# Preparation stage of a two-layer network: four places for contexts and heads, another order of the first loads, statistics split around the root

## The reference

```python
x = x + _L0_xattn_ref(_layernorm(x), ctx_512, ...)      # 16 heads
# in _L0_xattn_ref:
q_hk = (hidden_q @ Wq.T).reshape(b, s, H, K)
q_big = einsum('bshk,hkq->bshq', q_hk, w_kc_q)
kv_rope = kv_c * cos[None] + _rotate_half(kv_c) * sin[None]
q_r = einsum('bshq,hqr->bhsr', q_big, W_qr)
k_r = einsum('bld,hdr->bhlr', kv_rope, W_kr)
scores = einsum('bhsr,bhlr->bhsl', q_r, k_r);  attn = softmax(scores)
ctx_c = einsum('bhsl,bld->bhsd', attn, kv_rope)
out = einsum('bhsd,hkd->bshk', ctx_c, w_kc_kv).reshape(b, s, H * K) @ Wo.T
x = x + _L0_ffn_ref(_layernorm(x), ...)                 # ternary weights
x = x + _L1_xattn_ref(_layernorm(x), ctx_512, ...)      # causal attention
x = x + _L1_ffn_ref(_layernorm(x), ...)                 # 8 of 32 experts
```

## Time and profile before

| what | us |
|---|---|
| three runs | 1895.8, 1899.0, 1899.07 (median 1899.0) |
| the profiled execution | 1894.58 |
| its span | 1892.7 |
| `prepare` in it | 0 to 125.6 |
| busy in the span: TensorE, VectorE, ScalarE, GpSimd | 1615.2, 1223.4, 1058.8, 641.3 |

### The profile page before, as it was taken

The page is one execution under the profiler, slowest core; times in us unless marked ns, Lnnn a source line. Parts: engine busy times, 40 slices in busy tenths (PEclk is TensorE's granted clock), DMA queues, the critical chain, the costliest instruction groups (busy, mean ns, idle before and its releaser), DMA issues. The chain is left out here.

```text
span 1892.7 us, 36294 instructions
## 1 busy us (share of the span) xinstructions
PE 1615.2 (85%) x12180; PEld 1033.0 (55%) x12199; DVE 1223.4 (65%) x2744; ACT 1058.8 (56%) x2661; POOL 641.3 (34%) x479
## 2 busy tenths in 40 slices
PE   5588999999999889989998777655489999999993
PEld 4455656656646645545554455443356666666562
DVE  5666796796796787787787767766833333333332
ACT  3347846746746727565675776642645555555452
POOL 4523403403404400000000222211067777777672
PEclk7779999999999999999999998776589999999997
DMA  7730130130120139786677001011446665656536
GB/s 232 264 128 9 35 90 12 35 90 12 34 90 12 38 119 345 243 302 199 222 256 238 28 2 37 27 36 47 118 90 134 146 139 130 156 117 153 129 76 219
DMA packets 143366, 226.62 MB, mean 120 GB/s; under 512 B 37887, under 2 KB 93439, under 8 KB 143062
## 3 DMA queue, kind: packets, MB, share of 16 engines
q1 hardware_dynamic: 107190, 195.90, 32.7%
q0 software_dynamic: 29344, 21.29, 6.9%
q10 hardware_dynamic: 6656, 7.11, 1.1%
HBM read 175.00 MB, written 98.80 MB: 145 GB/s over the span
## 5 line engine op out<-in xcount | busy, mean ns | idle before, releaser
L2741 PE MATMUL g_ps<-ring,xT 128*128 x1572 | 300.7, 327 | 1.0 <-issue 1.0
L1012 POOL TENSOR_TENSOR pr<-pr,sm 100x1444 f32<-100x1444 f32 x64 | 166.2, 2596 | 367.9 <-DVE sm L1044 367.9
L2690 POOL DMA_INDIRECT acc<-rows,slot_sources x131 | 207.8, 1586 | 107.2 <-issue 77.0
L2847 DVE SCALAR_TENSOR_TENSOR hf<-sg,g_ps 128x192 f32<-128x192 f32 x131 | 46.4, 354 | 236.4 <-ACT sg L2796 189.0
L2741 PEld LDWEIGHTS g_ps<-ring,xT 128*128 128x128 f16 x1572 | 142.3, 98 | 72.3 <-issue 6.9
L2680 POOL DMA_INDIRECT xg<-xtab,slot_sources x131 | 138.4, 1056 | 81.8 <-issue 79.9
L1039 DVE TENSOR_REDUCE sm<-s_banks 100x2 f32<-100x722 f32 x128 | 115.8, 905 | 76.0 <-PE s_banks L783 75.5
L2763 PE MATMUL d_ps<-ring,hT 128*128 x655 | 162.8, 379 | 2.0 <-issue 1.3
L936 ACT ACTIVATE pr<-s_banks,sm 100x361 f32<-100x361 f32 x256 | 142.2, 567 | 34.1 <-DVE sm L1039 30.0
L783 PE MATMUL s_banks<-kvp,qp 128*100 128x361 f16 x768 | 138.6, 317 | 9.1 <-ACT pr L936 4.7
L840 PE MATMUL o_bank<-cT,N_hi 128*128 128x400 f16 x512 | 129.4, 335 | 1.9 <-ACT tern_a L615 0.8
(11 more groups left out here) (328 smaller groups left out, 3873.8 us busy)
## 6 DMA issues: line engine op xcount, KB each, us to landing
split_f<-in_gu SPq DMA_DIRECT2D x64, 384.0 KB, 4.5
split_gu<-split_o SPq DMA_DIRECT2D x64, 384.0 KB, 3.1
ring<-split_gu SPq DMA_DIRECT2D x32, 768.0 KB
head<-in_head SPq DMA_DIRECT2D x16, 864.0 KB, 6.4
tern_w<-in_tern SPq DMA_DIRECT2D x48, 256.0 KB, 3.2
split_f<-in_down SPq DMA_DIRECT2D x32, 384.0 KB, 4.2
split_d<-split_o SPq DMA_DIRECT2D x32, 384.0 KB, 3.7
ring<-split_d SPq DMA_DIRECT2D x32, 256.0 KB
```

The source lines that it names most:

```text
L1012: nc.gpsimd.tensor_tensor(pr[:, s % 3], pr[:, s % 3], small[:, s % 3, 2, :].unsqueeze(2).to_broadcast([SEQ, 4, KEYS]), ALU.mult).then_inc( ...
L2690: nc.gpsimd.indirect_dma_start(out=core.acc[i % NACC][:, :], out_offset=bass.IndirectOffsetOnAxis(ap=core.sources[:, i:i + 1], axis=0), in ...
L2741: last = nc.tensor.matmul(g_ps[i % 2][:, 0:2 * INTER], xT[:, i % 2, a * KT + k, :], ring(i, (2 * k + w) * 2 * INTER, 2 * INTER), start=((k ...
```

## The change

Contexts and heads get four places each (2 and 3 before). SP asks for rows of chunk 0 ahead of head 0, for those of chunk 1 behind context 2, and for those of chunk c+2 at b = 4c+1. A chunk's next statistics are split: `before_root` runs behind the moments in pass 2 of the chunk, the root stands ahead of `ln.high` on ScalarE in pass 3, and `after_root` is where the whole was. The moments stay.

```diff
--- before.py
+++ after.py
@@ -293,14 +293,14 @@
     core.gate = (w["gateT"], w["alpha"])
     assert BATCH == HEADS
     DQT = DCQ // P
-    NH = 3
+    NH, NK = 4, 4
     core.first_stage()
     x_even, x_odd, tab_in, kr_in = (core.sem(n) for n in ("x_even_in", "x_odd_in", "rope_tables_in", "kr_in"))
     kr_hi = core.sem("kr_hi_done")
 
-    kv_in = Slots(core, "kv_in", 2, per=16)
-    prod, roped = Steps(core, "rope_products", per=3, depth=2), Steps(core, "kv_roped")
-    lat_turned, turned = Steps(core, "latent_turned", depth=2), Steps(core, "kv_turned", depth=2)
+    kv_in = Slots(core, "kv_in", NK, per=16)
+    prod, roped = Steps(core, "rope_products", per=3, depth=NK), Steps(core, "kv_roped")
+    lat_turned, turned = Steps(core, "latent_turned", depth=NK), Steps(core, "kv_turned", depth=2)
     hi, lo = Steps(core, "kv_hi", per=3), Steps(core, "kv_lo", per=3, depth=2)
     saved = Slots(core, "kv_saved", 2, per=32, depth=1)
 
@@ -311,7 +311,7 @@
     with ExitStack() as ctx:
         cos = core.sb(ctx, "rope_cos", [P, 3, DC], F32)
         sin = core.sb(ctx, "rope_sin", [P, 3, DC], F32)
-        kv = core.sb(ctx, "kv_stage", [P, 2, 3, DC], F32)
+        kv = core.sb(ctx, "kv_stage", [P, NK, 3, DC], F32)
         a = core.sb(ctx, "rope_a", [P, 2, 3, DC], F32)
         s = core.sb(ctx, "rope_s", [P, 2, 3, DC], F32)
         r = core.sb(ctx, "kv_rope", [P, 2, 3, DC], F32)
@@ -345,10 +345,10 @@
 
             @block.sync
             def _(sp):
-                def load_context(b, p):
+                def load_context(b):
                     sp.wait_ge(lat_turned.sem, lat_turned.room(b))
                     sp.wait_ge(prod.sem, prod.room(b))
-                    sp.dma_start(kv[:, p], w["ctx"][b]).then_inc(kv_in[p].sem, 16)
+                    sp.dma_start(kv[:, b % NK], w["ctx"][b]).then_inc(kv_in[b % NK].sem, 16)
 
                 def load_head(h):
                     if h >= NH:
@@ -363,21 +363,26 @@
                     sp.dma_start(core.x_rows[:, c * CB:(c + 1) * CB, :],
                                  w["x"][c * CB:(c + 1) * CB].rearrange("b s d -> s b d")).then_inc(arrived, 16)
 
-                load_context(0, 0)
+                load_context(0)
                 sp.dma_start(cos[:, :, :], w["cos"]).then_inc(tab_in, 16)
                 sp.dma_start(sin[:, :, :], w["sin"]).then_inc(tab_in, 16)
+                load_rows(0)
                 load_head(0)
-                load_rows(0)
-                load_context(1, 1)
+                load_context(1)
                 load_head(1)
+                load_context(2)
+                load_rows(1)
                 load_head(2)
+                for h in range(3, NH):
+                    load_head(h)
+                load_context(3)
                 for b in range(BATCH):
-                    if b + 2 < BATCH:
-                        load_context(b + 2, b % 2)
+                    if b + NK < BATCH:
+                        load_context(b + NK)
+                    if b % CB == 1 and b // CB + 2 < NCH:
+                        load_rows(b // CB + 2)
                     if b + NH < BATCH:
                         load_head(b + NH)
-                    if b % CB == 0 and b // CB + 1 < NCH:
-                        load_rows(b // CB + 1)
                     if b == BATCH // 2:
                         sp.dma_start(kr[:, :, :], w["krT"]).then_inc(kr_in, 16)
                 for p in range(2):
@@ -393,12 +398,13 @@
                 for i in range(BATCH // 2):
                     for p in range(2):
                         b = i * 2 + p
-                        pool.wait_ge(kv_in[p].sem, kv_in[p].after(i))
-                        nc.gpsimd.tensor_tensor(a[:, p], kv[:, p], cos[:, :, :], ALU.mult).then_inc(prod.sem, 1)
-
-                        nc.gpsimd.tensor_tensor(s[:, p, :, 0:half], kv[:, p, :, half:DC], sin[:, :, 0:half],
+                        k = b % NK
+                        pool.wait_ge(kv_in[k].sem, kv_in[k].after(b // NK))
+                        nc.gpsimd.tensor_tensor(a[:, p], kv[:, k], cos[:, :, :], ALU.mult).then_inc(prod.sem, 1)
+
+                        nc.gpsimd.tensor_tensor(s[:, p, :, 0:half], kv[:, k, :, half:DC], sin[:, :, 0:half],
                                                 ALU.mult).then_inc(prod.sem, 1)
-                        nc.gpsimd.tensor_tensor(s[:, p, :, half:DC], kv[:, p, :, 0:half], sin[:, :, half:DC],
+                        nc.gpsimd.tensor_tensor(s[:, p, :, half:DC], kv[:, k, :, 0:half], sin[:, :, half:DC],
                                                 ALU.mult).then_inc(prod.sem, 1)
                         pool.wait_ge(prod.sem, prod.after(b))
                         pool.wait_ge(turned.sem, turned.room(b))
@@ -412,10 +418,11 @@
 
             @block.tensor
             def _(pe):
-                def turn_latent(i, b, p):
-                    pe.wait_ge(kv_in[p].sem, kv_in[p].after(i))
+                def turn_latent(b, p):
+                    k = b % NK
+                    pe.wait_ge(kv_in[k].sem, kv_in[k].after(b // NK))
                     pe.wait_ge(lo.sem, lo.room(b))
-                    nc.tensor.transpose(lat_cols(p), kv[0:SEQ, p, 0, :], core.ident[0:SEQ, 0:SEQ]
+                    nc.tensor.transpose(lat_cols(p), kv[0:SEQ, k, 0, :], core.ident[0:SEQ, 0:SEQ]
                                         ).then_inc(lat_turned.sem, 1)
 
                 def turn_keys(b, p):
@@ -448,7 +455,7 @@
                 pe.wait_ge(core.made, IDENT_MADE)
                 for n in range(BATCH):
                     p = n % 2
-                    turn_latent(n // 2, n, p)
+                    turn_latent(n, p)
                     turn_keys(n, p)
                     if n:
                         ln.turn(pe, n, p)
@@ -491,10 +498,10 @@
                 for n in range(BATCH):
                     p = n % 2
                     context_hi(n // 2, n, p)
+                    if n % CB == CB - 1 and n + 1 < BATCH:
+                        ln.root(act, n // CB + 1)
                     if n:
                         ln.high(act, n, p)
-                    if n % CB == CB - 1 and n + 1 < BATCH:
-                        ln.root(act, n // CB + 1)
                     inner_hi(n, p)
                     save_context(n, p)
                     outer_hi(n, p)
@@ -537,7 +544,7 @@
                     if bi < CB - 1:
                         ln.norm(dve, n + 1, 1 - p, bi + 1)
                     elif n + 1 < BATCH:
-                        ln.statistics(dve, c + 1, taken=True)
+                        ln.after_root(dve, c + 1)
                         ln.norm(dve, n + 1, 1 - p, 0)
 
                 for n in range(BATCH):
@@ -556,6 +563,8 @@
                         dve.wait_ge((x_odd, x_even)[c % 2], 16 * ((c + 1) // 2 + 1))
                         for j in (2 * bi - 2, 2 * bi - 1):
                             ln.moments(dve, (c + 1) * CB + j, j)
+                        if bi == 2:
+                            ln.before_root(dve, c + 1)
                     if n == BATCH - CB - 1:
                         dve.wait_ge(kr_hi, 1)
                         nc.vector.scalar_tensor_tensor(core.kr_lo[:, :, :], kr[:, :, :], KR_SCALE,
```

## The result

Before: median 1898.45 us (1895.8 to 1899.07). Changed: median 1883.51 us (1880.32 to 1886.34). The ratio is 0.9918 with a 95% interval of 0.9900 to 0.9936, that is 12 to 19 us faster. The forecast was 1880 us, with a range of 1869 to 1892.

A forecast was written before the change was run, and what follows sets the result against it. Late loads in bursts were taken to hold up the first stage. -21.1 + 4.9 - 3.2, with 2 us given back, made -17.4: 1894.6 to 1877.2, plus 2.8 for the median, 1880 us; eight in ten from 1869 to 1892.

The forecast's parts named there:

- Part 1: First stage: four context places and earlier rows of x remove TensorE's context waits and both holes; 21.1 us gained.
- the lower bound of 10.5: First stage, earlier loads: the bursts only move and half the waits stay; 10.5 us gained.
- the sentence on what hides the loads: First stage: the rest of it hides the loads, DMA share 82% against 0.87 where TensorE is not held up.
- Part 2: First pass: head 0 waits behind rows of chunk 0, so the pass starts 4.9 us later.
- The landing at 7.8: Start of stage, before the change: head 0, issued at 3.0, lands 4.8 us later, at 7.8.
- the rows' 2.9 us at 279 GB/s: First pass, low bound: rows ahead of head 0 take 2.9 us; it lands at 10.7, 0.8 us lost.
- Part 3: Chunk ends: split statistics let ScalarE's root run sooner, 1.06 us gained three times, 3.2 us.
- The 8.4 us at the upper end of its range: Chunk ends: upper end for the split statistics; TensorE waits 8.4 us at three places for ScalarE's g.
- The 2 us given back: First stage: 2 us off the gain, for dense loads and VectorE work about as long as a fast pass.
- Rival 1: First stage: loads are the bound, holes fill with other waits, half of Part 1 and Part 3 remains; 1890 us, 17%.
- Rival 2: First stage: the clock stays up, against granted 0.63 and 0.72 in and after the first hole; 14%.
- Rivals 3 and 4: First pass: head 0 waits, nothing comes back, 1902 us, 5%; or another limit at the same places, 1897 us, 6%.

The follow-up runs named there:

- e2: The changed kernel without the split of the statistics, all small VectorE operations together at the chunk end; 1889.2 us, ratio 0.9954 to the kernel before.
- e11: The kernel before with only rows of x of chunk 0 asked for ahead of head 0; 1897.4 us, ratio 1.0019.
- e12: The changed kernel with four places for saves and without the split of the statistics; 1878.3 us, ratio 0.9914 to the kernel before.
- e1: The changed kernel with head 0 asked for ahead of rows of chunk 0 again; 1880.5 us, ratio 0.9919 to the kernel before.
- e6: The changed kernel with four places instead of two for saved split contexts; 1876.7 us, ratio 0.9894 to the kernel before.
- e10: The changed kernel with head 0 first, four save places, GpSimd held before context 2 until first rows are normalised; 1873.3 us, ratio 0.9907.

## Why the prediction was right, and where its terms were not

**The total.** -17.4 was forecast for the stage; it was -15.0 in the traces and -14.9 in the medians.

**Where it is won.** Right: everything comes from the first stage; no wait for rows and, on TensorE, none for contexts after pass 0; and no hole over 4 us (TensorE's longest wait after 30 us is 3.0). Rest and stage were kept apart correctly: the forecast has no term for the rest, and the 2.9 us seen there lie in a scatter of 11.

**Part 1, "So TensorE's waits for contexts and rotated contexts go, both holes with them": 21.1 us.** The waits went, but not the time. Compare passes of e2 (parts 1 and 2) with e11 (part 2): 101.4 to 91.2, which is 10.2 us, about the lower bound of 10.5. Most of the other half turned into a wait that I never priced, as the 8.4 us show that e12 wins on e2 with more places for saves. ScalarE needs its save buffers back after two passes, and without the holes it comes back for them sooner than a save lands. The save issued at 54.84 lands 10.5 us later, and pass 7 stands:

```profile
54.84 0.54 ACTq L473 DMA_DIRECT2D lat_parts<-lat_parts_sb  x1
...
63.99 0.25 DVE L222 TENSOR_SCALAR ln_t<-ln_t 100x4 f32<-100x4 f32 x1
65.41 0.52 ACT L478 ACTIVATE kv_parts_sb<-kv_rope 128x384 f16<-128x384 f32 x1 [4.88 <-DMA lat_parts<-lat_parts_sb]
...
66.35 0.21 ACT L238 ACTIVATE ln_t<-ln_t 100x4 f32<-100x4 f32 x1
...
66.83 0.23 ACT L487 ACTIVATE g<-gc_ps 128x64 f32<-128x64 f32 x1
```

The small operations were through at 64.24 and the root could have run then; it waited for its turn behind the save until 66.35. With four places for saves (e12 against e11) part 1 is 101.4 to 82.8, 18.6 us: most of the 21.1. The failing step is the sentence on what hides the loads: I compared shares of the DMA engines (0.82 against 0.87) and left out who waits for the transfers in the other direction. A mean share told nothing of this landing: it is 0.78 over the stage, and 1.02 in 55:65, while the save is under way. The landings were hardly shorter before: 10.4 us at the most (in pass 0), and 9.8 and 9.7 in the two holes, where nobody was in a hurry. What holds a landing back for 10 us is not shown; no run here tells an order among the transfers from a plain share of the engines.

**Part 2, 4.9 us.** Mechanism right, size high. Head 0 was used at 14.0 in the mean (14.8 forecast). But the reference of 10.12 is at the low end of 10.0 to 11.5 over eight traces, so the delay at g 0 is 3.3. The landing at 7.8 was misread besides: 4.8 us is the shortest of all sixteen heads, and head 0's own was 6.3 in that trace, so it landed at 9.3. From there the rows' 2.9 us at 279 GB/s would give 12.2 and not 10.7 for the lower bound. (The 6.6 MB of the start are 6.4 by the sizes of the loads; nothing hangs on it.) And the chain behind it is not rigid: it contains VectorE operations that GpSimd stretches or not depending on when they fall (0.85 us against 0.17 in e1). Alone the edit costs 3.6 us in time (e11); in the changed kernel undoing it brings nothing that can be measured (e1). With GpSimd held as well and four places for saves the stage ends 3.7 us before e6's in the traces (e10), but not in time.

**Part 3, 3.2 us.** The sum of operations was right for a kernel whose saves are in time: 2.9 (e12 against e6). In the changed kernel it is 7.9 in the trace, 6.8 in time by the ratios, because it also puts the root's inputs ahead of the late save. The 8.4 us at the upper end of its range are the whole wait for g of the earlier trace rows; no run shows a gain of that size from the operations alone. Part 1's shortfall and part 3's surplus are in large part two sides of one wait. That, and part 2's lower price, is why the total came out near with two of three terms off by more than half. The sum was luckier than its terms.

**The 2 us given back** are probably too little for what fills the stage now: TensorE waits for the norm 6.9 us over eight times after 30 us, GpSimd for VectorE 24.0. No run prices them alone.

**Rivals.** Rival 1 (the loads are the bound) has the right half of the mechanism: half of part 1 was lost, but to saves and not to loads, and two more buffers win most of it back. Rival 2 (the clock stays up) can't be put aside, and its share is open. By the earlier trace rows a pass is 6.1 us long where its weight loads take 1.40 and 3.6 where they take 0.75. The granted clock of the stage rose from 0.76 to 0.85, and the same 384 matmuls keep TensorE busy for 72.5 us instead of 77.8. In the weight loads for g each pass shows its level (1.35 or 1.40 us slow, 0.75 fast; passes 4 and 5 of the changed kernel, where the granted clock is 0.50 from 47 to 51 us and 1.00 from 51 to 55):

```profile
47.59 1.40 PEld L439 LDWEIGHTS gc_ps<-head 128*128 128x128 f32 x6
...
52.42 0.75 PEld L439 LDWEIGHTS gc_ps<-head 128*128 128x128 f32 x6
```

Wholly slow passes fell from eight to five, wholly fast ones rose from seven to eight, and the rest lie between. So up to 5.3 of the 15.0 us can be the clock, and up to 6.4 of part 1's 10.2 (TensorE busy 77.3 us in e11, 70.9 in e2). The forecast has no term for that, and no run separates it from the waits that went. Rivals 3 and 4 are refuted by the traces.

## What to carry to other kernels

When loads are moved forward into a gap, list everything that used the gap, stores too: a double-buffered store that never waited can become the next bound (11.9 us of waits in the changed kernel), and one more buffer pair can take that wait away (0 in e6). Price each edit in the kernel in which it will stand; here the split of the statistics was worth 8, 3 or 0 us depending on its neighbours. Where a chain of tiny VectorE operations is on the path (5.9 us in e1, 3.3 in e10), look at what GpSimd does in those microseconds before speeding up what leads there.

## What the hardware showed that was not expected

An operation on 4 columns takes 0.17 us or 0.85, depending on what GpSimd does beside it (e1, e10); in e1 the twelve small ones and the norm take 5.9 us, in e10 3.3. And SP's issues took long at the start: in the changed kernel the two head loads issued at 6.33 us, behind nine other loads, occupy SP for 5.42 us, where the one at 19.43 takes 0.33. In e1 it is 5.24 us for the same two, and in the kernel before 1.12 for two behind six others. Why they take long was not tested.

```profile
6.33 5.42 SPq L357 DMA_DIRECT2D head<-in_head  x2
```

What SP was to issue next waited with it. That was context 3, for which GpSimd idled 6.7 us, until 29.35; TensorE never waited for it, so no loss of the stage is seen from it.
